# A graph layer with layer norm: pair loads, filler matmuls and the order of group 0's lead-in

## The reference

```
msg = relu(x[src] + edge_attr)            # one row for each edge
agg = segment_sum(msg, dst, 50000)
h   = relu((x + agg) @ W1 + b1) @ W2 + b2 # 128 -> 256 -> 128
out = layernorm(x + relu(h))              # over the 128 features
```

## Time and profile before

| | us |
|---|---|
| three runs: median (lowest to highest) | 459.33 (459.14 to 460.5) |
| the profiled execution, its own time | 459.34 |
| its span, first to last instruction | 457.7 |
| PE busy | 450.5 |
| DVE busy | 433.3 |
| ACT busy | 394.6 |
| POOL busy | 370.1 |

### The profile page before, as it was taken

One profiled execution on the slowest core, in us unless ns is written; L12 is line 12 of the kernel. 1 busy time (PEld: TensorE's weight loads), 2 busy tenths in 40 slices (PEclk: granted clock), 3 DMA queues, 4 the chain that ended last, 5 costly groups with the idle time before them and its releaser, 6 DMA issues.

```text
span 457.7 us, 10675 instructions
## 1 busy us (share of the span) xinstructions
PE 450.5 (98%) x3046; PEld 380.4 (83%) x3046; DVE 433.3 (95%) x1759; ACT 394.6 (86%) x930; POOL 370.1 (81%) x403
## 2 busy tenths in 40 slices
PE   8999999999999999999999999999999999999995
PEld 7888888888888888888888888888888888888884
DVE  6899999999999999999999999999999999999996
ACT  3599888888888889988888888888888888888886
POOL 7778888888888878778888888888888888888842
PEclk9999999999999999999999999999999999999998
DMA  5576666666566666666666666666666666666632
GB/s 135 164 234 199 201 187 201 194 195 203 181 197 202 181 199 202 185 192 200 197 205 190 201 190 195 194 194 200 198 195 197 186 199 202 185 203 191 196 126 90
DMA packets 83870, 86.82 MB, mean 190 GB/s; under 512 B 12023, under 2 KB 79508, under 8 KB 83812
## 3 DMA queue, kind: packets, MB, share of 16 engines
q1 hardware_dynamic: 75044, 68.77, 48.2%
q0 software_dynamic: 8496, 17.38, 14.1%
q10 hardware_dynamic: 272, 0.00, 0.0%
HBM read 60.51 MB, written 25.60 MB: 188 GB/s over the span
## 4 chain that ended last, share of the span: by engine, by line
PE 98%; DVE 1%; ACT 0%; POOL 0%; issue 0%; DVEq 0%; POOLq 0%
PE h_ps L1052 38%; PE h1T_ps L1044 36%; PE hT_ps L965 11%; PE hT_ps L960 9%; PE h1T_ps L464 1%; PE prep_ps L451 0%; DVE stats L696 0%; PE hT_ps L936 0%; PE hT_ps L953 0%; DVE z L689 0%; PE h1T_ps L1032 0%; ACT std L851 0%; PE hT_ps L454 0%; ACT h1T L846 0%; PE h1T_ps L1025 0%
## 5 line engine op out<-in xcount | busy, mean ns | idle before, releaser
L135 POOL DMA_INDIRECT x_src<-in_x_dram,src_of x254 | 270.3, 1064 | 65.5 <-issue 59.8
L1052 PE MATMUL h_ps<-w_sb,h1T 128*128 128x128 f32 x1564 | 197.5, 276 | 0.0
L1044 PE MATMUL h1T_ps<-hT,w_sb 128*128 128x384 f32 x520 | 188.5, 485 | 0.0
L1052 PEld LDWEIGHTS h_ps<-w_sb,h1T 128*128 128x128 f32 x1564 | 185.2, 192 | 0.0
L846 ACT ACTIVATE h1T<-h1T_ps,b_sb 128x384 f32<-128x384 f32 (+1 forms) x262 | 151.5, 579 | 35.4 <-PE h1T_ps L1044 27.1
L1044 PEld LDWEIGHTS h1T_ps<-hT,w_sb 128*128 128x128 f32 x520 | 88.7, 191 | 34.2
L865 ACT ACTIVATE y<-z,shift,rstd 128x128 f32<-128x128 f32 x263 | 114.6, 483 | 1.1 <-DVE shift L716 0.2
L596 POOL TENSOR_SCALAR y<-z,rstd,shift 128x128 f32<-128x128 f32 x123 | 87.7, 713 | 13.5 <-DVE shift L716 9.0
L965 PE MATMUL hT_ps<-sel,msg_hi 128*128 128x216 f32 x250 | 94.8, 447 | 0.0
L696 DVE BATCH_NORM_STATS2 stats<-z 128x6 f32<-128x128 f32 x391 | 88.6, 282 | 0.1
L960 PE MATMUL hT_ps<-ident,x_sb 128*128 128x128 f32 x375 | 87.5, 272 | 0.0
(11 more groups left out here) (139 smaller groups left out, 187.9 us busy)
## 6 DMA issues: line engine op xcount, KB each, us to landing
x_sb<-in_x_dram SPq DMA_DIRECT2D x130, 192.0 KB, 2.4
out_dram<-y SPq DMA_DIRECT2D x130, 192.0 KB, 2.4
pre_msg<-in_edge_attr_dram SPq DMA_DIRECT2D x130, 128.0 KB, 2.8
x_src<-in_x_dram,src_of POOLq DMA_INDIRECT x254, 3.0
w_sb<-in_w_dram SPq DMA_DIRECT2D x2, 128.0 KB, 2.6
dst_rows<-in_dst_dram SPq DMA_DIRECT2D x1, 97.7 KB
x_src<-in_x_dram,first_pairs POOLq DMA_INDIRECT x6, 2.8
b_sb<-in_b_dram SPq DMA_DIRECT2D x1, 64.0 KB, 3.3
```

The source lines that it names most:

```text
L135: nc.gpsimd.indirect_dma_start(out=c["x_src"][:, g % EB, k, :], out_offset=None, in_=x, in_offset=bass.IndirectOffsetOnAxis(ap=index, axis ...
L1044: nc.tensor.matmul(h1T_ps[h][:, 0:n, 0:p], w1_sb[:, h * 128:(h + 1) * 128], hT[:, 0:n, 0:p], start=True, stop=True).then_inc(h1_summed, 1)
L1052: last = nc.tensor.matmul(h2_ps[g % 2][0:p, t, :], h1T[:, h, t, 0:p], w2_sb[:, h, :], start=(h == 0 and t == 0 and not biased(g, c)), stop ...
```

## The change

- **Pairs.** The six chunks of `first_pairs` come by three DMAs, all on ACT's queue and ahead of its table load: chunk 0, chunk 1 (with a semaphore of its own), chunks 2 to 5. The one on SP's queue is gone. POOL waits for the second before gather 1; DVE waits for both before it copies the targets of chunks 0 and 1.
- **Filler.** A tile `filler` of ones is written by DVE's second instruction. PE waits for it in place of the identity, runs nine idle matmuls from it in place of seven, and waits for the identity after the matmuls of L451.
- **PE's order.** x of group 0 is turned for both banks, and the third boundary matmul (`find_ends`) runs, before the message sums of group 0. Then `hidden_part` comes ahead of `turn_starts` and `sum_whole`. The two halves of group 0's `output_sum` come ahead of and behind `sum_first(4)`, and `turn_windows` comes behind them (before, it was ahead of them).
- **DVE's order.** `count_start(0)` comes ahead of the first sum of group 0, and `low_part(0, 0)` ahead of `first_edges`.
- **ACT's order.** `copy_part` comes ahead of `whole_part`, `hidden(0, 0)` ahead of `high_part(1, 1)`, and `copy_hT(1)` ahead of `source_nodes`.

```
--- before.py
+++ after.py
@@ -196,6 +196,7 @@
     sums_ps = prep_ps[0][0:1, R:R + FLAGS]
 
     ones_col = sb("ones_col", [128, 1])
+    filler = sb("filler", [128, 128])
     row_of = sb("row_of", [ROWS, 1])
     lowest = sb("lowest", [ROWS, 1])
     highest = sb("highest", [ROWS, 1])
@@ -228,11 +229,13 @@
     next_loaded = sem("next_loaded")
     first_loaded = sem("first_loaded")
     pairs_loaded = sem("pairs_loaded")
+    second_pairs_loaded = sem("second_pairs_loaded")
     more_pairs_loaded = sem("more_pairs_loaded")
     first_dst_ready = c["first_dst_ready"]
     w1_loaded, w2_loaded = c["w1_loaded"], c["w2_loaded"]
     pool_consts = c["pool_consts"]
     ident_ready = sem("ident_ready")
+    filler_ready = sem("filler_ready")
     vec = sem("vec")
     eps_ready = sem("eps_ready")
     dst_f_ready = sem("dst_f_ready")
@@ -254,8 +257,6 @@
         sp.dma_start(dst_rows[:, :], dst.rearrange("(r e) -> r e", e=ROW)).then_inc(dst_loaded, 16)
         start_edge_attr(sp, edge_attr, 0, 0, c)
         start_x(sp, x, 0, 0, c)
-        sp.dma_start(first_pairs[:, 2:FIRST_CHUNKS, :], pairs[2 * EW:FIRST_CHUNKS * EW, :].rearrange("(k p) a -> p k a", p=EW),
-                     allow_slow_non_contiguous=True).then_inc(more_pairs_loaded, 16)
         start_edge_attr(sp, edge_attr, 1, K * EW, c)
         sp.dma_start(c["w1_sb"][:, :], w1).then_inc(w1_loaded, 16)
         for h in range(HC):
@@ -292,6 +293,7 @@
 
         pool.wait_ge(pairs_loaded, 16)
         start_first_gather(nc, x, 0, c)
+        pool.wait_ge(second_pairs_loaded, 16)
         start_first_gather(nc, x, 1, c)
         pool.wait_ge(more_pairs_loaded, 16)
         start_first_gather(nc, x, 2, c)
@@ -394,6 +396,7 @@
 
     def prepare_vector(dve):
         nc.vector.memset(dst_next[:, :], 0).then_inc(next_cleared, 1)
+        nc.vector.memset(filler[:, :], 1.0).then_inc(filler_ready, 1)
         nc.vector.memset(eps_col[:, :], LN_EPS).then_inc(eps_ready, 1)
         nc.vector.memset(ones_col[:, :], 1.0)
         nc.vector.memset(c["ones_row"][:, :], 1.0).then_inc(c["ones_row_ready"], 1)
@@ -419,6 +422,7 @@
         link(dve, nc.vector.tensor_tensor(first_of[:, :], dst_first[:, :], lowest[:, :], ALU.min))
         link(dve, nc.vector.tensor_scalar(row_before[:, :, :], node_row[0:ROWS, :, :], first_of[:, 0:1], None, ALU.is_gt))
         dve.wait_ge(pairs_loaded, 16)
+        dve.wait_ge(second_pairs_loaded, 16)
         nc.vector.tensor_copy(first_dst[:, 0:2], first_pairs[:, 0:2, 1]).then_inc(first_dst_ready, 1)
         dve.wait_ge(pool_consts, 5)
         dve.wait_ge(first_dst_ready, 1)
@@ -431,8 +435,9 @@
 
     def prepare_scalar(act):
 
-        act.dma_start(first_pairs[:, 0:2, :], pairs[0:2 * EW, :].rearrange("(k p) a -> p k a", p=EW),
-                      allow_slow_non_contiguous=True).then_inc(pairs_loaded, 16)
+        for k0, k1, loaded in ((0, 1, pairs_loaded), (1, 2, second_pairs_loaded), (2, FIRST_CHUNKS, more_pairs_loaded)):
+            act.dma_start(first_pairs[:, k0:k1, :], pairs[k0 * EW:k1 * EW, :].rearrange("(k p) a -> p k a", p=EW),
+                          allow_slow_non_contiguous=True).then_inc(loaded, 16)
         act.wait_ge(eps_ready, 1)
         nc.scalar.activation(table_mark[:, :], eps_col[:, :], ACT.Sqrt)
         act.wait_ge(dst_loaded, 16)
@@ -442,17 +447,20 @@
 
     def prepare_tensor(pe):
 
-        pe.wait_ge(ident_ready, 1)
-        keep_busy(7)
+        pe.wait_ge(filler_ready, 1)
+        keep_busy(9)
         pe.wait_ge(dst_f_ready, 1)
         pe.wait_ge(row_of_ready, 1)
         pe.wait_ge(row_holds_ready, 1)
         for k in range(K):
             nc.tensor.matmul(found_ps[k], row_holds[:, k, :], dst_rows_f[:, 0:ROW + 1], start=True, stop=True).then_inc(row_found, 1)
+        pe.wait_ge(ident_ready, 1)
         pe.wait_ge(c["x_loaded"][0], 16)
-        for t in range(T):
-            nc.tensor.matmul(c["hT_ps"][:, t, :], c["x_sb"][:, 0, t, :], ident[:, :], is_transpose=True,
-                             start=(t == 0), stop=False, skip_group_check=True)
+        for ps in (c["hT_ps"], c["h2_ps"][1]):
+            for t in range(T):
+                nc.tensor.matmul(ps[:, t, :], c["x_sb"][:, 0, t, :], ident[:, :], is_transpose=True,
+                                 start=(t == 0), stop=False, skip_group_check=True)
+        find_ends(pe)
 
     def find_ends(pe):
 
@@ -461,7 +469,7 @@
     def keep_busy(times):
 
         for _ in range(times):
-            nc.tensor.matmul(c["h1T_ps"][0][:, 0, :], ident[:, :], ident[:, :], start=True, stop=True)
+            nc.tensor.matmul(c["h1T_ps"][0][:, 0, :], filler[:, :], filler[:, :], start=True, stop=True)
 
     def turn_starts(pe):
 
@@ -469,7 +477,7 @@
         nc.tensor.matmul(starts_ps, window_start[:, 0:1], ident[0:R, 0:R], start=True, stop=True).then_inc(starts_summed, 1)
 
     return dict(sync=prepare_sync, gpsimd=prepare_gpsimd, vector=prepare_vector, scalar=prepare_scalar, tensor=prepare_tensor,
-                find_ends=find_ends, turn_starts=turn_starts, count_start=count_start, first_edges=first_edges,
+                turn_starts=turn_starts, count_start=count_start, first_edges=first_edges,
                 split_edges=split_edges, start_edges=start_edges, check_ends=check_ends,
                 find_order=find_order, check_order=check_order, check_limits=check_limits, find_targets=find_targets,
                 check_targets=check_targets, set_general=set_general, sum_flags=sum_flags)
@@ -723,11 +731,11 @@
             return nc.vector.tensor_scalar(y[0:p, g % YB, t, :], z[0:p, g % ZB, t, :], rstd[0:p, g % SB, t:t + 1],
                                            shift[0:p, g % SB, t:t + 1], ALU.mult, ALU.add)
 
+        checks["count_start"](dve, 0)
         add_edge_attr(0, 0)
-        checks["count_start"](dve, 0)
         checks["count_start"](dve, 1)
+        low_part(0, 0)
         checks["first_edges"](dve)
-        low_part(0, 0)
         checks["split_edges"](dve)
         add_edge_attr(0, 1)
         checks["start_edges"](dve)
@@ -866,19 +874,19 @@
                                         bias=shift[0:p, g % SB, t:t + 1], scale=rstd[0:p, g % SB, t:t + 1])
 
         high_part(0, 0)
+        copy_part()
         whole_part(0, 1)
-        copy_part()
         high_part(0, 1)
         copy_rest()
         high_part(1, 0)
         act.wait_ge(c["starts_summed"], 1)
         nc.scalar.activation(c["starts_row"][:, :, 0:1].rearrange("a g k -> a (g k)"), c["prep_ps"][0][0:1, 0:R],
                              ACT.Copy).then_inc(c["starts_row_ready"], 1)
+        hidden(0, 0)
         high_part(1, 1)
-        hidden(0, 0)
         hidden(0, 1)
+        copy_hT(1)
         source_nodes()
-        copy_hT(1)
         high_part(2, 0)
         hidden(1, 0)
         high_part(2, 1)
@@ -1000,11 +1008,7 @@
             pe.wait_ge(c["first_sel_ready"], 1)
             pe.wait_ge(msg_hi_ready, 1)
             add(hT_ps, 0, FIRST_PART, msg_hi)
-            for t in range(T):
-                nc.tensor.matmul(rest_ps[:, t, :], x_sb[:, 0, t, :], ident[:, :], is_transpose=True,
-                                 start=(t == 0), stop=False, skip_group_check=True)
             add(rest_ps, FIRST_PART, 128, msg_hi)
-            checks["find_ends"](pe)
             pe.wait_ge(msg_lo_ready, 1)
             add(hT_ps, 0, FIRST_PART, msg_lo).then_inc(part_summed, 1)
             add(rest_ps, FIRST_PART, 128, msg_lo)
@@ -1055,20 +1059,20 @@
                 last.then_inc(h2_summed, 1)
 
         sum_first_parts()
+        pe.wait_ge(c["w1_loaded"], 16 * (1 + HC))
+        hidden_part()
         checks["turn_starts"](pe)
         sum_whole(1)
-        pe.wait_ge(c["w1_loaded"], 16 * (1 + HC))
-        hidden_part()
         turn_x(1)
         hidden_rest()
         sum_first(2)
         sum_first(3)
+        pe.wait_ge(c["w2_loaded"], 16)
+        output_sum(0, 0)
         sum_first(4, final=True)
+        output_sum(0, 1)
         pe.wait_ge(c["starts_row_ready"], 1)
         turn_windows(nc, pe, src_ps, dst_ps, c)
-        pe.wait_ge(c["w2_loaded"], 16)
-        output_sum(0, 0)
-        output_sum(0, 1)
         hidden_sum(1)
         turn_x(2)
         for i in range(5, 8):
```

54 lines of the change are left out of this document (29 added, 25 removed).

## The result

The changed kernel takes 461.93 us (median; 461.72 to 464.03, 7 runs) against 459.49 us (7 runs) for the kernel before: 2.44 us more, a ratio of 1.0059 with the interval 1.0047 to 1.007. The forecast was 459.6 with a range that ended 1.2 above the kernel before, so the result lies outside. The profiled execution took 462.13 with a span of 460.5, 2.8 more than the 457.7 of before.

A forecast was written before the change was run, and what follows sets the result against it. PE, 98% busy, was taken as the bound, with three lead-in chains meeting near 19.7 us. Plus 0.35 on the gathers' chain, minus 0.05 for gather 0, gave plus 0.3: 459.6 us, range minus 0.6 to plus 1.2.

The forecast's parts named there:

- The path: Late-turned windows delay group 3's second gather and its sum, so PE waits at sum_messages(3): plus 0.35 us.
- price of 0 for the pairs: Start: ACT's extra issue and DVE's added wait are covered; price 0, packets beside dst_rows bounded minus 0.1 to plus 0.4.
- sum of group 3: DVE's sum after group 3's second gather: forecast at 18.6 us, 0.35 later than the 18.25 before.
- hidden_rest 11.2: PE, end of group 0's first hidden layer: forecast 11.2 us, against 11.46 before.
- PE's own gain: PE's lead-in to the end of hidden_rest: 0.26 us earlier, the rest eaten by the hidden part moved ahead of sum_whole.
- I take 3.0: Group 3's second gather, issued at 15.6: lands 3.0 us after issue, the median, because fewer loads stand beside it.
- The upper bound named, 3.7: Group 3's second gather: at most 3.7 us from issue to landing, which would give 19.3.
- The starts: DVE's window starts after group 0's first sum come about 0.1 us earlier, bounds 0 to 0.3.
- The clock rival: TensorE keeps its lower level until about 8 us, hidden_rest ends at 12.05, giving 460.5 us; chance 0.15.
- The faster rival: Gather 3 lands within 2.7 us, or gather 0 comes 0.2 to 0.3 earlier, giving 459.0 us; chance 0.25.

The follow-up runs named there:

- Wide filler: Changed kernel with three idle matmuls of 384 columns in place of its nine of 128, 24 instructions fewer: 460.91 us, ratio 1.0026.
- the other cut into three: Kernel before with all pairs on ACT's queue as chunks 0 and 1, chunk 2, chunks 3 to 5, no further wait: 460.27 us, ratio 1.002.
- The run with the rise near 10 us: Kernel before with nine idle matmuls from the identity (five of 128 columns, four of 64) in place of seven, eight instructions more: 460.85 us, ratio 1.0024.

## Why the prediction was wrong

**The path was right, its terms were not.** The windows turned late feed the second gather of group 3, that feeds the sum, and PE waits there. The measured chain goes through these steps in this order, and putting the windows back takes 1.75 of 2.44 away. Being 98% busy, PE left nothing to win later. What failed is the size of two terms of that path and the price of 0 for the pairs. In the span, 2.22 of the 2.8 came by the path, where the forecast had 0.35, and 0.6 came behind group 3, where the forecast had nothing.

**Term by term, sum of group 3.** Forecast 18.6, measured 20.47, 1.87 later. Three terms make it:

- "hidden_rest 11.2": measured 12.08, 0.88 later. Copy_part was put near 8.0 and came at 8.51. The turned starts and sum_whole were put at up to 0.76 together and took 0.89, with their start at 9.77 instead of 9.1 to 9.2; the copy behind them and `hidden_rest` itself (1.00 in place of 0.73 plus 0.25) came as forecast. With this, the gather went out at 16.49 instead of 15.6, 0.89 late. That PE's own gain would be 0.26 is wrong: in the changed order it stands idle while ACT copies (the wait of 0.4 at L1029), and no part of sum_whole covers that any more.
- "I take 3.0": the landing took 3.89, 0.89 more. The upper bound named, 3.7, was also too low. It was read from a kernel where the load stands near the end of the gather, so it was a bound for that place and not for a later one. The reason given for 3.0, fewer loads beside it, did hold where PE's load let the gather pass: in the four traces in which it was issued at 15.7 to 16.8 and not held up, it took 2.6 to 3.1. Wide filler, which moves PE's load, takes 1.04 off the time of the changed kernel.
- The remaining 0.09 lies between landing and sum.

**"Price 0" for the pairs** failed. They cost 0.76 alone and 1.1 to 1.2 within the change, where the windows' chain has no slack left. In the kernel before, the wait on DVE, which the step looked at and found covered, was indeed not the price, as the other cut into three showed. Within the change it was not covered: `row_holds`, behind that wait, ends at 5.29 in place of 4.56, and the row matmuls start at 5.43 in place of 5.10 in the timelines of PE; with the windows first, PE idles 0.3 for `row_holds`. The pieces that the traces show are 0.41 of lead-in within the change (12.08 against 11.67), which that start explains for the most part, and the stall of 0.4 near 157 us, which lies outside the stretch that the forecast looked at. The step also said that what small packets do beside dst_rows was not shown anywhere and bounded it at plus 0.4; that was too narrow. The Trainium skill ("DMA: Bandwidth & Descriptors", section "Issuing engines are not separate DMA queues") says that transfers interleave on the same engines. The landing of gather 0 agrees in direction only: the first sum runs at 6.76 to 7.40 in the seven kernels with all pairs on ACT's queue and at 6.27 to 7.01 in the other thirteen, so it scatters too much to give a price.

**The starts.** Foreseen 0.1 earlier; the window gather went out at 8.78, 0.19 later than 8.59, since the row matmuls ended at 7.11 in place of 6.87 and the counts behind them moved with them.

**The clock rival** named a time of 12.05 for `hidden_rest`, and 12.08 was measured, but not for its reason. The transposes take 0.39 for three from 7.11, so the higher level came at about 7, later than the 6.5 that the rival named as its condition. With the windows first, in contrast, where PE has the same work up to 8 us, the filler records shorten from 0.21 to 0.11 at 4.2. PE waited there for the high part until 7.74 (0.5 idle between 7 and 8), gather 0 at 6.87 set the pace, and `hidden_rest` ended at 11.93, 0.15 earlier. Its first sum was 0.13 later than in the changed kernel. As far as these two traces tell, an early rise would have given 0.15 to 0.3 and no more, so the clock accounts for about a third of the 0.88 at most. The run with the rise near 10 us shows that a later rise does cost, 0.7 us. The rise lay elsewhere from trace to trace. The Trainium skill ("TensorE: Matmul & The Clock Gate", Part 1) says that it varies from run to run; the traces agree, and here it varied by almost 3 us between two kernels with the same work ahead of it.

**The faster rival** asked for a landing under 2.7 or a gather 0 that comes sooner; the opposite was measured of both. The filler costs nothing that can be seen as work: with wide matmuls it is plus 0.12. As nine narrow ones it costs 0.67, and its trace shows the load at 16.78 in the gather and PE waiting 1.0 behind it.

**What stays open.** The way from the third transfer to the stall near 157 us, and to one of about 0.2 near 211 us, is not known; together they are 0.6 of the 2.8 in the span. Why the gathers of group 3 issued before 15.3, that of the filler kernel with wide matmuls among them, took up to 4.0 with the load behind them is not known either, nor which part of the 1.04 is the load's and which the chance of a gather that passes it. The parts do not add up (windows 1.75, pairs 1.21, wide filler 1.04 of 2.44), because each only counts where the others have used up the slack.

## What to carry to other kernels

A landing time read from one trace holds for that moment of the run; when a change shifts a gather by one or two microseconds, look in the short DMA stretches for what it will now share its 16 engines with, the instruction stream among it. Price what a split transfer adds to the queues and not only the waits that it adds: three transfers with every wait covered cost 0.84 us, and two 0.29. Where several chains meet within 0.05 us, price a move on every one of them, and test the price with the other costs taken away.

## What was not expected of the hardware

PE's instruction stream comes over the same 16 DMA engines as the data, in packets of 16 KB that hold one of them for 1.05 to 1.4 us in the three read above. When such a packet begins 0.5 to 2.0 us after the issue of a gather, the gather takes 4.0 us in place of 3.0 (medians of 244 and 1792 gathers in twenty traces), and in five gathers of group 3 the last piece came 1.1 to 1.2 us after the packet's end. Twenty-four instructions of filler fewer moved the load from 18.15 to 19.02 and took 1.0 us from the time of a kernel of 460. That the wait for the gather goes when the load moves was shown in two kernels (the changed one, and the one with the filler alone). In the one with the windows late the wait went with the load in its place, and the one attempt to put a load into a gather did not move it there. Every kernel with three small transfers on ACT's queue at 2 us has a stall of 0.4 us near 157 us, and none with two or one; the cause is open.
